# Moving low halves, results and the gate's exponential at the turn of the passes

## What is computed

```
x = x + tanh(g_xattn) * attention(layernorm(x), ctx)
xf = layernorm(x)                        # 1792 tokens x 512
logits = xf @ gate_w.T + gate_b          # 8 per token
logits = logits * rsqrt(mean(logits**2) + eps) * rms_w
g = max(softmax(logits / 0.5))
norm_g = g / (g + 1e-6)
h = gelu(xf @ w1[e] + b1[e])             # for e in 0..7, 512 -> 1024
y = h @ w2[e] + b2[e]                    # 1024 -> 512
out = x + tanh(g_ffn) * norm_g * sum_e y
```

## Time and profile before

| | us |
|---|---|
| median of three runs | 1900.96 (1900.19 to 1901.15) |
| profiled execution, its own time | 1901.04 |
| its span | 1899.3 |

### The profile page before, as it was taken

One profiled execution on the slowest core, in us unless ns is written; L12 is line 12 of the kernel. 1 busy time (PEld: TensorE's weight loads), 2 busy tenths in 40 slices (PEclk: granted clock), 3 DMA queues, 4 the chain that ended last, 5 costly groups with the idle time before them and its releaser, 6 DMA issues.

```text
span 1899.3 us, 32919 instructions
## 1 busy us (share of the span) xinstructions
PE 1830.2 (96%) x10360; PEld 1653.1 (87%) x10360; DVE 1321.5 (70%) x2247; ACT 814.4 (43%) x1570; POOL 1183.0 (62%) x901
## 2 busy tenths in 40 slices
PE   5999999999999878999999999999999999999998
PEld 5999999999999867888888888887888888888887
DVE  6777777777777667767666666679776676666657
ACT  4676676766766553323223233233233232232322
POOL 5435254452535378877777777867877777777743
PEclk9999999999999988999999999999999999999999
DMA  5002111010200203211212111113312112121111
GB/s 172 18 23 68 29 42 50 21 55 27 60 29 26 81 28 121 67 56 55 66 45 66 58 52 66 56 52 110 112 56 67 55 55 66 44 66 56 54 45 50
DMA packets 51803, 110.38 MB, mean 58 GB/s; under 512 B 12952, under 2 KB 25240, under 8 KB 51744
## 3 DMA queue, kind: packets, MB, share of 16 engines
q1 hardware_dynamic: 51744, 109.63, 18.3%
HBM read 98.61 MB, written 11.01 MB: 58 GB/s over the span
## 4 chain that ended last, share of the span: by engine, by line
PE 84%; DVE 8%; issue 4%; ACT 3%; DMA 0%; ACTq 0%; DVEq 0%; SPq 0%
PE bank L683 30%; PE scores L658 27%; PE bank L537 16%; PE scores L601 4%; PE bank L624 3%; PE bank L611 3%; DVE xs L777 1%; DVE acc L944 1%; DVE queries L841 1%; DVE neg_max L860 1%; ACT queries L1057 1%; DVE probsT L777 1%; ACT keys L1057 1%; PE bank L544 1%; DVE acc L957 1%
## 5 line engine op out<-in xcount | busy, mean ns | idle before, releaser
L683 PE MATMUL bank<-w2s,hs 128*128 128x512 f32 x2688 | 621.8, 390 | 5.6 <-DVE acc L944 5.6
L683 PEld LDWEIGHTS bank<-w2s,hs 128*128 128x128 f32 x2688 | 504.2, 188 | 110.2 <-DVE acc L944 7.7
L658 PE MATMUL scores<-xs,w1s 128*128 128x448 f32 x2688 | 562.1, 367 | 4.1 <-DVE h_sum L923 4.1
L658 PEld LDWEIGHTS scores<-xs,w1s 128*128 128x128 f32 x2688 | 507.5, 189 | 49.0 <-issue 2.8
L923 DVE TENSOR_TENSOR h_sum<-scores,h_sum 128x448 f32<-128x448 f32 x448 | 267.0, 619 | 190.9 <-PE scores L658 190.5
L944 DVE TENSOR_TENSOR acc<-bank,acc 128x512 f32<-128x512 f32 x434 | 295.6, 687 | 124.7 <-PE bank L683 115.5
L1183 ACT ACTIVATE h_full<-h_sum,b1T 128x448 f32<-128x448 f32 x256 | 170.9, 668 | 316.6 <-DVE h_sum L923 306.3
L777 DVE TENSOR_TENSOR hs<-h_full,hs 128x448 fp32r<-128x448 f32 x256 | 236.1, 923 | 50.6 <-ACT hs L1184 50.6
L1057 ACT ACTIVATE h_sum<-scores 128x448 f32<-128x448 f32 x64 | 34.9, 545 | 490.6 <-PE scores L658 490.4
L1244 POOL TENSOR_SCALAR probs<-probs,row_inv 112x750 f32<-112x750 f32 x64 | 140.9, 2202 | 164.9 <-DVE row_inv L866 164.9
L1339 POOL CAST w1s<-w_stage 128x768 fp32r<-128x768 f32 x64 | 67.8, 1059 | 183.1 <-PE scores L658 183.1
(11 more groups left out here) (112 smaller groups left out, 2128.5 us busy)
## 6 DMA issues: line engine op xcount, KB each, us to landing
w_stage<-in_L_ffn_w SPq DMA_DIRECT2D x128, 512.0 KB, 3.5
ctx_raw<-in_ctx SPq DMA_DIRECT2D x8, 752.0 KB, 4.7
ctx_raw<-in_ctx SPq DMA_DIRECT2D x7, 748.0 KB, 4.7
xa<-in_x SPq DMA_DIRECT2D x16, 224.0 KB, 2.9
xres<-in_x SPq DMA_DIRECT2D x16, 224.0 KB, 2.7
x_scratch<-xres SPq DMA_DIRECT2D x16, 224.0 KB, 2.3
xt_scratch<-yT SPq DMA_DIRECT2D x16, 224.0 KB, 2.9
x_raw<-xt_scratch SPq DMA_DIRECT2D x4, 896.0 KB, 6.0
```

The lines of the kernel that those rows point to most:

```text
L658: mm = pe.matmul(mb[BANK_OF[name]][:, 0:TH], w1s[j % 2][:, s, W_OF[name], kc, :], xs[:, i, m, kc, :], start=n == 0, stop=n == 5)
L683: mm = pe.matmul(bank[:, :], hs[j % 2][:, s, ht, t * P:(t + 1) * P], w2s[j % 2][:, m, ht, :], start=n == 0, stop=n == 5)
```

## The change

1. ScalarE's exponential of the gate moves from behind the second gelu of step (p,7,2) to behind the fourth.
2. VectorE's last part of the gate moves from the end of the sums of (p,7,2) to step (p,7,3), behind U2.
3. The low halves i = 4, 5, 6 of the second pass's x are made by GpSimd, in its step (1,0,0) between `w1_part` of (1,0,1) and `split_w2` of (1,0,0), under a semaphore of their own. VectorE makes i = 0 to 3.
4. The results of pass 0 are spread over four steps: 0 and 1 behind i = 4 and 6 of (1,0,0), 2 behind i = 3 of (1,0,1), 3 and 4 behind i = 3 and 6 of (1,0,2), 5 and 6 behind i = 3 and 6 of (1,0,3). SP's x2 loads, stores and w2 loads follow; in each of these steps w2's load stands behind the step's first store.

```diff
@@ -41,6 +41,8 @@
 NS = len(SUMS)
 NM = len(MIX)
 TURN = (1, 0, 0)
+RESULTS = {(1, 0, 0): {4: 0, 6: 1}, (1, 0, 1): {3: 2}, (1, 0, 2): {3: 3, 6: 4}, (1, 0, 3): {3: 5, 6: 6}}
+POOL_LOWS = 4
 LN_EPS = 1e-5
 RMS_EPS = 1.1920928955078125e-07
 TEMPERATURE = 0.5
@@ -273,6 +275,7 @@
         yT_stored = [sem(f"yT_stored{i}") for i in range(2)]
 
         x_raw_loaded, x_mixed, x_hi, x_split = sem("x_raw_loaded"), sem("x_mixed"), sem("x_hi"), sem("x_split")
+        x_split_pool = sem("x_split_pool")
         b1_loaded, b2_loaded = sem("b1_loaded"), sem("b2_loaded")
         small_loaded, small_set = sem("small_loaded"), sem("small_set")
         w1_loaded, w1_step, w1_split = sem("w1_loaded"), sem("w1_step"), sem("w1_split")
@@ -309,6 +312,10 @@
 
         def at(g, there):
             return isinstance(g[1], int) and g == there
+
+        def results_of(g):
+
+            return RESULTS.get(g, {}) if isinstance(g[1], int) else {}
 
         def early(g, back):
 
@@ -499,24 +506,25 @@
                 then = after and following(after)
                 if then:
                     load_w1(then)
-                if after and not (g[0] == 1 and isinstance(g[1], int) and g[1] == 0 and g[2] < 2):
+                if after and not results_of(g):
                     load_w2(after)
                 if at(g, (0, 0, 1)):
                     sp.wait_ge(x_split, NM)
                     load_x_raw(1)
-                if at(g, TURN) or at(g, (1, 0, 1)):
-                    for k in (range(4), range(4, PT))[g[2]]:
+                if results_of(g):
+                    for n, k in enumerate(results_of(g).values()):
                         if k + XB < PT:
                             load_x2(k + XB)
                         store_out(0, k)
-                        if k == (2, 5)[g[2]]:
+                        if n == 0:
                             load_w2(after)
                 if at(g, (0, NE - 1, 2)):
                     sp.wait_ge(gate_tr, 1)
                     for k in range(XB):
                         load_x2(k)
                 if at(g, (1, 0, 3)):
-                    sp.wait_ge(x_split, NP * NM)
+                    sp.wait_ge(x_split, NM + POOL_LOWS)
+                    sp.wait_ge(x_split_pool, NM - POOL_LOWS)
                     sp.dma_start(x2_last, x2_scratch.rearrange("b q d -> (b q) d")[PT * P:, :].rearrange(
                         "(t p) d -> p t d", p=P)).then_inc(x2_last_loaded, 16)
 
@@ -645,7 +653,10 @@
                     if at(g, (0, 0, 0)):
                         pe.wait_ge(exp_out, 16 * B)
                 if at(g, (p, 0, 0)):
-                    pe.wait_ge(x_split, p * NM + i + 1)
+                    if p and i >= POOL_LOWS:
+                        pe.wait_ge(x_split_pool, i - POOL_LOWS + 1)
+                    else:
+                        pe.wait_ge(x_split, p * NM + i + 1)
                 last_reader = {"P1": (-1, "V"), "P6": (-1, "C12"), "P2": (-1, "C21"),
                                "P7": (0, "U2"), "P4": (0, "C11"), "P3": (0, "U3")}.get(name)
                 if last_reader and not (last_reader[0] and early(g, 1)):
@@ -972,7 +983,7 @@
                         h_low(g, t + 2)
                     if at(before or g, (0, NE - 1, JS - 2)) and t in (2, 4, 6):
                         split_x(1, t // 2 - 1)
-                    if at(before or g, (0, NE - 1, JS - 1)) and t in (0, 2, 4, 6):
+                    if at(before or g, (0, NE - 1, JS - 1)) and t % 2 == 0 and t // 2 + 3 < POOL_LOWS:
                         split_x(1, t // 2 + 3)
 
             def batch(name, plan, b):
@@ -1037,12 +1048,12 @@
                     tiles(None, previous(g))
                 for i in range(NM):
                     sums(g, i)
-                    if closing and j == 2 and i in (0, 2, 6):
-                        gate(p, (0, 2, 6).index(i))
-                    if at(g, TURN) and i % 2 == 0:
-                        result(0, i // 2)
-                    if at(g, (1, 0, 1)) and i % 2:
-                        result(0, 4 + i // 2)
+                    if closing and j == 2 and i in (0, 2):
+                        gate(p, i // 2)
+                    if closing and j == 3 and i == 1:
+                        gate(p, 2)
+                    if i in results_of(g):
+                        result(0, results_of(g)[i])
                 tiles(g, None if at(g, TURN) else previous(g))
 
             steps(dve, step, (0, 0, 1))
@@ -1208,7 +1219,7 @@
                         if p:
                             act.wait_ge(out_ready, PT)
                         copy(gate_lt[:, half * TH:(half + 1) * TH], mb[3][0:16, 0:TH]).then_inc(gate_copied, 1)
-                    if closing and j == 2 and i == 4:
+                    if closing and j == 2 and i == 6:
                         act.wait_ge(gate_step, GATE_STEPS * p + 10)
                         act.activation(logits_tmp[:, :, :], logits[:, :, :], ACT.Exp,
                                        scale=1.0 / TEMPERATURE).then_inc(gate_exp, 1)
@@ -1387,6 +1398,11 @@
                 if after and not at(g, (0, 0, 0)):
                     for k in range(5):
                         w1_part(after, k)
+                if at(g, (1, 0, 0)):
+                    for i in range(POOL_LOWS, NM):
+                        pool.wait_ge(x_hi, NM + i + 1)
+                        pool.tensor_tensor(xs[:, i, 1], x_source(i), xs[:, i, 0].bitcast(F32),
+                                           ALU.subtract).then_inc(x_split_pool, 1)
                 split_w2(g)
                 if at(g, (0, 0, 1)):
                     for qt in range(2):
```

## The result

The changed kernel takes 1896.8 us (median of 11, 1892.5 to 1898.7) against 1901.15 of the kernel before beside it: the ratio is 0.9973, 95% interval 0.9965 to 0.9981, and the medians are 4.3 us apart. The changed kernel's profiled execution took 1894.48 (span 1892.7), the fourth fastest of the eleven, and 1.2 us of that lie ahead of the edited steps: the second phase of step (0,7,2) starts at 1260.86 instead of 1262.02, in code that is the same.

What follows compares the result with a forecast made beforehand. TensorE, busy 96% of the span, was taken as the bound, with 13.4 us lost near the edits. From 1901.04, gains of 3.0 (second pass), 1.0 (first pass) and 0.8 (turn) gave 1896.2, range 1890.5 to 1898.8.

Steps and rivals of the forecast that it cites:

- Edits 1 and 2, second pass: Steps (1,7,2) and (1,7,3): the 3.1 us loss goes, 0.1 left over, gain 3.0 (2.0 to 3.1).
- one or two waits take 2.4 to 4.2: Gate's six moved operations with waits for GpSimd: C11 done at 6.3 to 8.1, a gap of 0.2 to 2.
- First pass: Gate gain in (0,7,2), partly repaid at the fifth tile and fourth split: 1.0 kept of 3.1 us (0 to 3.1).
- Edit 3: Turn step (1,0,0): the 2.47 us gap and 1.8 of clock behind it go; GpSimd's low halves, 2.12 each, stay hidden.
- Edit 4 and the new gap: Before the fourth product of (1,0,1): gap of 4.0 us, clock falls again, 1.8; turn gain 0.8 (-1 to 6.6).
- its own sign: Gap before the fourth product of (1,0,1) should be 3 to 4.6 us; prediction wrong if under 2.
- T: Time at which the products of the turn step (1,0,0) start, 1302.22 before, some 1301.2 expected.
- case B: Turn waits fall better: gap stays but clock holds, 1894.4, chance 0.20; or only 0.4 lost, 1890.7, chance 0.12.
- case A: The forecast itself: turn gap near 4 us with the clock falling once, 1894.5 to 1898, chance 0.50.
- Results in later steps: Low halves, results and add-ups jammed in (1,0,1) to (1,0,3): 0.4 us lost (0 to 3).
- Case D: Slower: five results in (1,0,1) to (1,0,3) each behind a whole GpSimd subtraction, 1904.1, chance 0.05.
- Case C: First pass's gate gain all repaid, turn's gap as long as the two before: 1.6 gained, 1899.4, chance 0.13.

Runs made afterwards that it cites:

- g_only: Edits 1 and 2 alone on the kernel before, low halves and results unchanged: 1899.56 us, ratio 0.9997 (0.9988 to 1.0006).
- pool_wait: Changed kernel with GpSimd held in step (1,0,1) until VectorE has made U2 of (1,0,1): 1894.29 us, ratio 0.9971 to the kernel before.
- lr_only: Edits 3 and 4 on the kernel before, the gate left as before: 1896.64 us, ratio 0.9976 (0.9967 to 0.9986).
- l_only: Edit 3 alone on the kernel before, gate and results unchanged: 1898.02 us, ratio 0.9986 (0.9978 to 0.9995).
- r_only: Edit 4 alone on the kernel before, gate and low halves unchanged: 1898.05 us, ratio 0.9987 (0.9979 to 0.9996).
- all3: Changed kernel with the gate's last part behind the tiles of (p,7,3), GpSimd held until U2 of (1,0,1), four low halves on GpSimd: 1899.73 us.
- lows3: Changed kernel with a fourth low half, i = 3, on GpSimd too: 1893.79 us, ratio 0.9970 to the kernel before.

## Why the prediction was right, point by point

Forecast 1896.2, range 1890.5 to 1898.8; measured 1896.8. The sum came out by luck: of its three terms one fell short by 2.1, one by 0.6, and the third was too low by 3.3.

- **Edits 1 and 2, second pass: the step that failed.** Gain 3.0 with 0.1 left over was forecast; the profiled execution gained 0.9. The prediction said that GpSimd has only w2 to split there and took that for free. But it was w2's copy and the 2.37 us subtraction behind it that held up two of the six operations (1863.39 and 1863.50), which took 4.3 us together. The prediction had that case in "one or two waits take 2.4 to 4.2" and didn't count it in the second pass; 0.9 also lies below its range of 2.0 to 3.1. g_only and pool_wait show that the other outcome, no loss, also occurs.
- **First pass: right in mechanism, a little high.** Forecast 1.0 kept of 3.1, measured 0.4. The six operations took 2.4 us, with one wait. C12 of (0,7,3) starts at 1283.89 in the changed kernel, 23.03 us after the second phase of (0,7,2) began, and at 1285.06 before, 23.04 after: the 3.1 us that TensorE gained did not move it at all against the start of that phase. The gap before the fifth tile was 0.25 (0.5 forecast) and the late add-up behind the fourth split, 2.68 us, made one of 1.40 (1.3 forecast). g_only and lr_only show the exchange: with the gate edits the joined phases lose 2.3 or 2.4, without them 0.
- **Edit 3: right.** The gap of 2.47 and the clock's fall behind it are gone in l_only, lr_only and the changed kernel, and no product waits for GpSimd's low halves, which take 2.96, 2.13 and 2.14 (2.12 forecast).
- **Edit 4 and the new gap: right in what makes it, wrong in its size and in the clock.** Low halves behind GpSimd's instructions set it, which pool_wait shows. Forecast were 4.0 us in one gap and 1.8 for the clock; measured 0.85 + 1.75 with 0.5 of drains, and no fall of the clock. The prediction called itself wrong if the gap before the fourth product of (1,0,1) is under 2 us: it is 1.75, so by its own sign this step failed. Its other signs held: no gap of 1.53 in (p,7,2), none at the fourth product of (1,0,0), no product waiting for GpSimd, no gap over 2 in (0,7,3). The prediction overlooked that the second product of (1,0,1) needs C12's bank, which breaks the gap in two, and took a full alternation for T between 1299.8 and 1302, while the low half at T + 5.9 took only 0.79 and result 0 0.86. The turn gained 4.1, not 0.8. The profiled execution looks like case B, the waits falling better and the clock holding. That its 1894.4 is also that execution's time, 1894.48, is chance: case B kept the gap of 4.0, and 1.2 us of the measured time was won ahead of the edits. The median of 11 lies at case A's time, which no trace explains.
- **Results in later steps: right.** Forecast 0.4 lost, measured 0.03 in (1,0,2) and nothing in (1,0,3). Case D fell: r_only is not slower. Case C's own sum was loose: it takes the turn to lose 1.4 more than before, below the prediction's bound of -1 for that term.
- **What the other executions do** was not seen: the profiled one is 2.3 us faster than the median. The coin of 0.05 us in the second pass can't be why, since there the profiled execution had the bad side; the good side would be 2.2 us faster still. The clock is a candidate: the six executions with a mean granted clock of 0.990 took 1892.5 to 1896.9 us, 1894.8 on average, and the five with 0.989, the median one among them, 1896.8 to 1898.7, 1897.6 on average. One fall as in r_only's two windows below (0.34 and 0.50 of 2 us missing) lowers the mean over 1893 us by 0.0009, an estimate. That fits one more fall in the longer executions; where it comes, no trace shows.

## What to carry to other kernels

When work goes from VectorE to GpSimd, price it not by its own length but by what it puts beside VectorE's two-operand instructions that stand in front of an awaited result: each can cost up to a whole GpSimd instruction, however few columns it has. Look for the place where that happens, and hold GpSimd there if it has slack; a hold of 4 us freed 1.2 at the turn and cost 0.8 two steps on. Read the steps behind the one you mend, too. And when a stall goes, ask what sets the next event: if its time doesn't follow the stalled engine, the gain is repaid there.

## What the runs showed of the hardware

- A VectorE instruction with both operands in SBUF waits until the running GpSimd instruction ends, and this stands in its duration, not as idle time: 2.28 us for seven columns, 0.67 in pool_wait; 1.17 or 0.61 for the same low half. The add with a constant waits too (1.01, 1.87), and GpSimd's copy (1.04) holds it as its subtraction does. The two take turns: between GpSimd instructions in a row one such VectorE operation each got in (1.87, 1.75, 2.00 in all3). Not all wait: beside GpSimd's subtractions a reciprocal on seven columns keeps its 0.20 (at 1298.23 in all3) and an add-up, with one operand in PSUM, its 0.6 to 0.7 (four in 2.48 at 1302.28). The Trainium skill, "SBUF — State Buffer", section "🔬 SBUF: two separate sides", has an exclusive lock held for the whole instruction. The rows agree with it.
- The clock's fall to the lower level does not go by a gap's length alone. In r_only a gap of 1.83 us is followed by windows at 0.66 and 0.50:

```profile
1306.00:1308.00 2.00, 1.96 (x7) 1.79 (x8) 0.42 (x1) 1.23 (x2) 0.00 (x0) 0.66 0.00 0
1308.00:1310.00 2.00, 2.00 (x7) 1.78 (x6) 1.16 (x2) 0.00 (x0) 0.00 (x0) 0.50 0.00 0
```

  In the changed kernel gaps of 0.85 and 1.75 close together left it at 1.00, in g_only one of 2.88 did not lower it in the windows behind and one of 1.78 after it is followed by 24 matmuls in 6.70 us instead of 5.13. In the second pass a gap of 1.94 was followed by 12 matmuls in 2.69 in the changed kernel, one of 1.88 by 12 in 3.81 in lows3. Each of these falls costs 1.6 to 1.8 us, about as much as the gap itself.
- A load of the activation table takes 1.28 us and comes behind the wait of the instruction that needs it: in the changed kernel 4.34 us of idle time and then the load, at 1276.80. It stood in front of VectorE's low half in (p,7,3), 2.15 us of its idle time, and cost TensorE nothing that the rows show: with it in place the second pass of g_only and pool_wait loses nothing.
